# Keys' low half, LayerNorm statistics, four bias additions and unread products moved in the attention stage of a decoder layer

## What is computed

```python
# attention, on h = layernorm(x); 8 heads, 64 tokens to a sequence
c_q, c_kv = h @ W_DQ + b_DQ, h @ W_DKV + b_DKV          # 32 wide
q = concat(c_q @ W_UQ + b_UQ, c_q @ W_QR + b_QR)        # by head
k = concat(c_kv @ W_UK + b_UK, h @ W_KR + b_KR)
attn = softmax(einsum('bhsd,bhtd->bhst', q, k) * scale)
o = einsum('bhst,bhtd->bhsd', attn, c_kv @ W_UV + b_UV)
x = x + o.reshape(b, s, -1) @ W_O + b_O
# experts 1: router on the context, inputs layernorm(x)
logits = einsum('bsd,de->bse', context, Wg) + bg        # top 2 of 8, softmax
...
x = x + out
# experts 2: 8 of 32 from 4 of 8 groups, and shared ones
...
x = x + routed + shared
```

## Time and profile before

| what | value |
|---|---|
| median of three runs | 731.56 us (730.13 to 733.31) |
| profiled execution | 733.41 us, its span 731.6 us |
| PE busy | 651.0 us (89% of the span) |
| DVE busy | 548.4 us (75%) |
| ACT busy | 347.3 us (47%) |
| POOL busy | 345.7 us (47%) |
| mean granted clock of PE | 0.958 |

### The profile page before, as it was taken

One profiled execution on the slowest core, in us unless ns is written; L12 is line 12 of the kernel. 1 busy time (PEld: TensorE's weight loads), 2 busy tenths in 40 slices (PEclk: granted clock), 3 DMA queues, 4 the chain that ended last, 5 costly groups with the idle time before them and its releaser, 6 DMA issues. The chain is left out here.

```text
span 731.6 us, 10978 instructions
## 1 busy us (share of the span) xinstructions
PE 651.0 (89%) x3408; PEld 457.8 (63%) x3408; DVE 548.4 (75%) x1321; ACT 347.3 (47%) x633; POOL 345.7 (47%) x400
## 2 busy tenths in 40 slices
PE   8967888786669999999982998999999999999997
PEld 8635555554657777777761755666666666666664
DVE  4777888889248999999964786877868695958564
ACT  3845577653025666666663434344343435253221
POOL 5223787777758999999956423050403122000000
PEclk9978999999889999999995999999999999999999
DMA  8900130000133566676211474454544545353442
GB/s 215 381 27 1 46 93 30 33 30 38 44 101 112 168 178 204 179 196 178 79 58 44 99 164 118 111 138 115 135 114 123 142 122 138 90 141 110 128 115 58
DMA packets 74871, 84.13 MB, mean 115 GB/s; under 512 B 15345, under 2 KB 43995, under 8 KB 74814
## 3 DMA queue, kind: packets, MB, share of 16 engines
q1 hardware_dynamic: 69688, 74.93, 37.1%
q0 software_dynamic: 4288, 8.40, 3.9%
q10 hardware_dynamic: 838, 0.11, 0.1%
HBM read 64.48 MB, written 18.87 MB: 114 GB/s over the span
## 5 line engine op out<-in xcount | busy, mean ns | idle before, releaser
L883 ACT ACTIVATE r_s<-bank 128x512 f32<-128x512 f32 x136 | 81.0, 597 | 149.6 <-PE bank L1457 136.9
L1677 PE MATMUL pair_banks<-t_s,Dn 128*128 128x512 f32 x272 | 137.9, 592 | 0.7 <-issue 0.7
L1192 DVE TENSOR_TENSOR h1l<-r,h1h 128x512 fp32r<-128x512 f32 x92 | 113.0, 1246 | 18.1 <-POOL h1h L610 18.1
L1307 DVE TENSOR_TENSOR rc_s<-r_s,score_banks 128x512 f32<-128x512 f32 x90 | 61.5, 683 | 47.9 <-ACT r_s L883 29.5
L1455 PE MATMUL bank<-fxh,Gh 128*128 128x512 f32 x136 | 95.1, 699 | 0.0
L1320 DVE TENSOR_TENSOR t_s<-rc_s,bcb 128x512 f32<-128x512 f32 x128 | 87.4, 685 | 3.7 <-DMA bcb<-c_rows 3.0
L610 POOL TENSOR_SCALAR h1h<-r 128x512 fp32r<-128x512 f32 x92 | 73.5, 803 | 21.7 <-ACT r L829 19.7
L629 POOL TENSOR_TENSOR mvp<-mvp,meps 128x4 f32<-128x4 f32 x8 | 1.6, 197 | 170.0 <-DVE mvp L1230 170.0
L549 POOL DMA_INDIRECT x_sorted<-xsb,posi x64 | 63.6, 994 | 28.3 <-DVE xsb L1106 15.3
L621 POOL DMA_INDIRECT yg<-y_sorted,posi x64 | 62.9, 983 | 24.9 <-issue 18.4
L1677 PEld LDWEIGHTS pair_banks<-t_s,Dn 128*128 128x128 f32 x272 | 51.4, 190 | 16.0 <-issue 5.0
(11 more groups left out here) (295 smaller groups left out, 1575.2 us busy)
## 6 DMA issues: line engine op xcount, KB each, us to landing
bcb<-c_rows SPq DMA_DIRECT2D x128, 256.0 KB
wraw<-in_L_xattn_W SPq DMA_DIRECT2D x46, 256.0 KB
x_sorted<-wraw SPq DMA_DIRECT2D x1, 5888.0 KB, 19.1
xg<-x_sorted SPq DMA_DIRECT2D x23, 256.0 KB, 3.5
y_sorted<-ysb SPq DMA_DIRECT2D x23, 256.0 KB, 3.0
ctxb<-in_ctx SPq DMA_DIRECT2D x8, 256.0 KB, 4.6
out<-x_all SPq DMA_DIRECT2D x8, 256.0 KB
x_all<-in_x SPq DMA_DIRECT2D x2, 512.0 KB, 6.1
```

Of the source, the lines that this page charges most:

```text
L883: act.activation(r_s[:, n % RB2, :], bank[n % 3][:, :], ACT.Silu).then_inc(F["act"], 1)
L1192: tt(h1l[:, n % NB1, :], r1[:, n % RB1, :], h1h[:, n % NB1, :].bitcast(F32), ALU.subtract)\
L1307: tt(rc_s[:, n % CB2, :], r_s[:, n % RB2, :], bank[3 + n % 3][:, :], ALU.mult).then_inc(F["rc"], 1)
L1677: mm(bank[6][:, :], Dn[:, weights_of(p), :], t_s[:, n % TB2, :], start=(p == 0), stop=(p == NC2 - 1))\
```

## The change

- `kvlo` has offset -4 instead of -3 and stands behind `maximum` in the step, ahead of the context copy, the statistics, the router's piece and the bias. For group 1 it stood ahead of the maximum of n = 0 and now stands behind it. It waits for `kvS` alone (a new semaphore `kvs`), and PE's keys wait for the second copy as well.
- The statistics of tiles 16 to 31, which stood at n = -1, 0, 5 and 6, stand at n = -4, -3, -2 and -1. There is one part for them instead of two, so one power on POOL less. It stands ahead of the loop.
- `load_x(2)` goes ahead of the output weights, and both behind the small loads; the second half of the context comes after them.
- The bias addition of groups 0 to 3 goes from DVE (n = 4, 8, 12, 16) to POOL (n = 4 to 7).
- The unread products at the start are 5, 2 and 3 instead of 14, 4 and 8. Four new ones stand at n = 2.
- The lags stay as they are.

```diff
@@ -54,16 +54,17 @@
 HEAD = dict(xn=((-12, 0), (-11, 1), (-9, 2), (-9, 3)), xT=((-7, 0),), xh=((-6, 0),), xl=((-6, 0),), kv=((-5, 0),),
-            cq=((-5, 0),), kvS=((-4, 0),), cqS=((-3, 0),), kvlo=((-3, 0),),
+            cq=((-5, 0),), kvS=((-4, 0),), cqS=((-3, 0),), kvlo=((-4, 0),),
             keys=((-3, 0), (-3, 1), (-2, 2), (-2, 3)), kst=((-2, 0), (-2, 1), (-1, 2), (-1, 3)), v=((0, 0),), vh=((1, 0),))
...
 TAIL = 10
+PB = 4
 NV = NT - 3
...
 CTX = dict(turn=(-6, -4, -3, -2), copy=(-4, -3, -2, -1), product=(-3, -2, -1, 0), read=(-2, -1, 0, 1), back=(1, 2))
-PARTS = ((0, 4), (4, 8), (8, 16), (16, 24), (24, 32))
+PARTS = ((0, 4), (4, 8), (8, 16), (16, 32))
@@ -317,7 +318,7 @@
         A = {n: sem("at_" + n) for n in (
-            "xn xo xT xh xl kv_ps kvh kv cq_ps cq k_ps kst v_ps vh s_ps max sm exp sum rden p pv pT_ps ph "
+            "xn xo xT xh xl kv_ps kvs kvh kv cq_ps cq k_ps kst v_ps vh s_ps max sm exp sum rden p pv pT_ps ph "
             "u_ps uh o_ps x1 bst mva eps rstd xs").split()}
@@ -370,14 +371,14 @@
                 load_ctx(i)
-            sp.dma_start(wo_a[:, :, :], W_O.rearrange("(h k) d -> k h d", h=H)).then_inc(s_wo, 16)
             for dst, src in ((wg_a[:, 0:E1], Wg), (brow[:, :], row(bg)), (gbrow[:, :], row(gate_bias)),
...
                 sp.dma_start(dst, src).then_inc(s_small, 16)
+            load_x(2)
+            sp.dma_start(wo_a[:, :, :], W_O.rearrange("(h k) d -> k h d", h=H)).then_inc(s_wo, 16)
             for i in range(4, NS):
                 load_ctx(i)
-            load_x(2)
             sp.wait_ge(s_ctx[NQ - 1], 32)
@@ -563,18 +564,26 @@
+            def add_out_bias(m):
+
+                pool.wait_ge(A["xn"], m + 1)
+                xr = x_all[:, m * TPS:(m + 1) * TPS, :]
+                pool.tensor_tensor(xr, xr, obb[:, :].unsqueeze(1).to_broadcast([P, TPS, D]), ALU.add).then_inc(A["xo"], 1)
+
+            rstd1(3)
             for n in range(NT + TAIL):
...
                     normalise_p(m)
-                if n == 1:
-                    rstd1(3)
-                if n == 7:
-                    rstd1(4)
-                    router1_positions()
+                if n == 4:
+                    pool.wait_ge(s_N, 2)
+                if 4 <= n < 4 + PB:
+                    add_out_bias(n - 4)
                 m = n - LAG["rstd"]
...
                     rstd_pair(m)
+                if n == 7:
+                    router1_positions()
                 m = n - LAG["scatter"]
@@ -723,7 +732,7 @@
                         act.wait_ge(s_bias, N_BIAS)
-                    act.activation(kvS[:, q, :], bank[2][:, :], ACT.Identity, bias=bkv[:, :])
+                    act.activation(kvS[:, q, :], bank[2][:, :], ACT.Identity, bias=bkv[:, :]).then_inc(A["kvs"], 1)
                     act.activation(ckvD[:, q, :, :, :], bank[2][0:DC, :].rearrange("p (b s) -> p b s", s=S).unsqueeze(2)
@@ -962,15 +971,14 @@
             def statistics_rest(n):
+                if n == -4:
+                    dve.wait_ge(s_xin[2], 16)
+                if -4 <= n <= -1:
+                    statistics(32 + 4 * n, 36 + 4 * n)
                 if n == -1:
-                    dve.wait_ge(s_xin[2], 16)
-                if n in (-1, 0, 5, 6):
-                    first = {-1: 16, 0: 20, 5: 24, 6: 28}[n]
-                    statistics(first, first + 4)
-                if n in (0, 6):
-                    variance_eps(3 if n == 0 else 4)
-                if n in (3, 8):
-                    negated_mean1(3 if n == 3 else 4)
+                    variance_eps(3)
+                if n == 2:
+                    negated_mean1(3)
@@ -1075,8 +1083,6 @@
-                if m == 0:
-                    dve.wait_ge(s_N, 2)
                 dve.wait_ge(A["xn"], m + 1)
@@ -1088,7 +1094,7 @@
                 if name == "kvlo":
-                    dve.wait_ge(A["kvh"], m + 1)
+                    dve.wait_ge(A["kvs"], m + 1)
                     at = kvS[KV:2 * KV, q, :]
@@ -1133,11 +1139,6 @@
                     residual1(o)
-                if n == 0:
-                    head("kvlo", 1, 0)
-                for name, j, part in head_steps(n, ("kvlo",)):
-                    if j != 1:
-                        head(name, j, part)
                 if 0 <= u < NT:
@@ -1161,13 +1162,13 @@
                     maximum(n)
-                for step in head_steps(n, ("xl",)):
+                for step in head_steps(n, ("xl", "kvlo")):
                     head(*step)
...
                 router1(n)
-                if n % TPS == 0 and 4 <= n < NT + 4:
+                if n % TPS == 0 and PB <= (n - 4) // TPS < NS:
                     add_out_bias((n - 4) // TPS)
@@ -1362,14 +1363,14 @@
             pe.wait_ge(s_ident, 1)
-            unread(bank[6], 14)
+            unread(bank[6], 5)
             pe.wait_ge(s_heads, 16 * 6)
-            unread(bank[6], 4)
+            unread(bank[6], 2)
             pe.wait_ge(s_hqk, 2)
@@ -1383,7 +1384,7 @@
             ins.then_inc(s_gps, 1)
-            unread(bank[6], 8)
+            unread(bank[6], 3)
@@ -1483,6 +1484,7 @@
                         pe.wait_ge(A["kv"], m + 1)
+                        pe.wait_ge(A["kvh"], m + 1)
                         if m == 0:
@@ -1582,6 +1584,8 @@
                     out_absorbed()
+                if n == 2:
+                    unread(bank[0], 4)
                 if n == 3:
...
                 if n == 5:
```

## The result

The changed kernel takes 728.7 us (median of 20 executions, 724.17 to 732.9) against 731.56 for the kernel before (20 executions, 730.13 to 735.15): a ratio of 0.9954 with a 95% interval of 0.9938 to 0.9970, so 3.4 us less (the two medians by themselves differ by 2.9). The forecast was 723.2, or 8.4 less. The direction and the range held; the likeliest case was more than twice too large. The profiled execution took 730.11 us (span 728.4); its counterpart took 733.41 (731.6). The ratios in this document leave out three executions in a slower state, one of 830 us (ten products, `fill_keys2`) and two of 739 (`fill_five`, the profiled one among them).

A forecast was written before the change was run, and what follows sets the result against it. PE was taken to set the pace from 20 to 38 us, DVE from 38 to 45 and 62 to 76, neither from 45 to 62. 5.6 us by n = 9 plus 2.8 steady made 8.4: 723.2 us, range 718.5 to 729.5.

The forecast's parts named there:

- Head: Start, up to the first key product: fewer unread products bring it 1.2 us earlier (bounds 0 and 2.5); first scores 0.2 late.
- first batch: Unread products at the very start, 14 cut to 5: at most 1.7 us gained, 0.5 net taken.
- Low half of group 1: n = 1 to 4: keys wait for the low half behind the maximum; 1.2 us later, with the head's 0.2 1.4 late.
- Low half of group 2: Ahead of the router's piece, near 50 us: low half 2.5 us earlier, less the 1.4, makes 1.1 early.
- The clock: PE from 45 to 62 us: full clock worth 3.5 us, no change 0; half taken, 1.8, so 2.9 early at n = 6.
- Statistics, positions: n = 5 to 9: statistics gone from DVE, one power off POOL, positions 1.8 earlier; together 2.0 to 3.5 us, 2.7 taken.
- Steady part: 80 to 176 us: PE's four waits for the keys' low half, 4.2 us in all, shrink; 2.8 us gained.
- The bias on POOL: n = 4 to 7, four additions of 1.04 us on POOL: zero effect, with 3.2 us for collisions with DVE in the range.
- (a): Rival: clock stays at half through the ranks and the stretch at 76, steady waits move elsewhere; 727.0 us, chance 0.17.
- (d): Rival: x load at n = -4 lands late and holds up copies, then PE; 727.0 us at landing 24.9, 736 at 34; chance 0.06.
- (b): Rival: POOL's scatter chain takes the pace from the first scatter on, nothing left of the steady 2.8; 726.0 us, chance 0.14.

The follow-up runs named there:

- fill_keys2: The changed kernel with ten more unread products on PE at n = 5, ahead of the keys of group 2: ratio 0.9880 to the kernel before.
- fill_five: The changed kernel with five unread products on PE at n = 5, ahead of the keys of group 2: ratio 0.9943 to the kernel before.
- three bias kernels: The changed kernel with all bias additions on DVE (0.9981), those of groups 4 to 7 left out (0.9917), or those one step later, ahead of the maximum (0.9910).
- low order alone: The kernel before with only the keys' low half of every group moved behind the maximum (offset -4): ratio 1.0054 to the kernel before.

## Why the prediction was right or wrong

**Head (1.2 earlier at the first key product): 0.7.** The landing was underrated (4.54, not 6), the slow clock was underrated more. No run shows the 0.5 that the sum takes for the first batch: PE started 3.1 us earlier and then needed 13.4 us to the first key product where it had needed 11.0, and in other traces of the same head this second number is 11.7 to 14.4. The copy of the context was foreseen behind the low half; I had its end at 21.1 and it came at 21.7. What that costs I had right: 1.4 us from the first key product to the first scores, measured 1.4 (14.80 us to the first maximum, before 13.37). So the first maximum came 0.7 late instead of 0.2 for the smaller gain ahead of it.

**Low half of group 1 (loop 1.4 late at n = 1 to 4): 2.1, then 3.1.** The first part by the mechanism told. The last 1.0 is the router's comparison beside POOL's bias. I had priced such meetings at zero with 3.2 in the range, on the ground that the steps next to it read PSUM. That one does not, and 1.0 was lost at once. Here the Trainium skill's rule (GPSIMD Engine Reference, Key points: GpSimd shares SBUF interfaces with VectorE and contends with instructions with two SBUF inputs) was the better guide; I had given it some 3 us and set it aside. The rows at 45.63 and 127.13 and those of the three bias kernels agree with it.

**Low half of group 2 (2.5 earlier).** Right as a term: from n = 4 to 5 the loop took 6.42 us where it took 8.82, 2.4 less.

**The clock (1.8): this step failed.** I took half of 3.5 for a partial cure and it was nothing: 9.14 us from n = 5 to 6, before 8.66. The reason given, that the gap shrinks from 3.56 to 2.9, fell with the late n = 4 (3.51 measured). It would not have been enough either: the gap is 1.61 us with the bias on DVE and 1.15 with the low order alone, and the key product behind it still takes 0.75 and 0.74, since the clock is down before the gap begins. The whole was mis-sized as well. With the fill, n = 0 to 6 takes 27.7 us instead of 32.1 (34.03 to 61.73, 32.76 to 64.87), 4.4 less where I had 3.5, and n = 6 to 9 takes 13.0 instead of 14.6, another 1.6. I had priced the keys, the ranks and the next round, not every pass up to n = 9.

**Statistics, positions (2.7): 1.9** from n = 6 to 9 (14.62 us, before 16.48). Right in kind. As one part alone it carries the whole result.

Together, n = 9: 0.7 + 1.3 + 1.0 - 2.4 + 0.5 - 1.9 = -0.8 (measured -0.7), where I had -5.6.

**Steady part (2.8): 0.6 by n = 31.** The waits did go: the steps 16 to 17 and 20 to 21 of PE's scores took 4.69 and 4.68 us, before 5.47, and 24 to 25 took 4.69, before 6.80. But steps 22 to 23 took 6.89 instead of 4.96 and 27 to 28 took 5.16 instead of 3.08. The step of the reasoning that failed was to count the waits of PE and not to ask where the instructions on DVE behind the moved one would land: the addition, 0.68 us alone, landed on POOL's normalisation and took 1.58, with POOL's scatter waiting for the scaling behind it. It is not all of the loss: 1.5 of the 1.9 us in step 22 to 23 is PE at its lower level, and so is much of step 27 to 28, where PE's rows are slow from 156.9 to 163. The prediction had no falls of the clock behind 80 us. With the additions ahead of the maximum the granted clock is 1.00 from 80 to 160 us.

**The bias on POOL (zero).** Zero alone (0.9994), but not in the new order: it costs 1.0 at n = 4 and spares collisions of DVE, for some 2 us net in its favour.

Of the rivals, (a) is what came about, by its two reasons at once: the clock stayed at half through the ranks, and the steady waits moved elsewhere. It gave 727.0; the collision at n = 4 (1.0) and the smaller gain at the head (0.5) make most of the rest. Rival (d), a late x load, didn't occur at all. (b), POOL's chain as pace setter, is not what the rows say: POOL still waited 12.4 us for DVE between 80 and 176:

```profile
POOL x_sorted L550 <- DVE xsb L1112: 12.4, 14, 2.5
```

**What stays open.** The changed kernel's executions spread over 8.7 us, those before over 5.0. The head's two courses can be a part of that: with the old numbers of unread products twelve executions spread over 5.1. Another cause can be read but was not tried by itself: in kernels that keep both of PE's new gaps (2.13 us at 21.75, 1.01 at 35.02), three of six traces have part of the half level between 33 and 42 us as well. The change and the kernel with the bias ahead of the maximum, in that stretch:

```profile
33.00:42.00 9.00, 7.20 (x62) 4.50 (x52) 6.91 (x15) 6.92 (x14) 3.29 (x2) 1.00 0.75 286
...
33.00:42.00 9.00, 7.98 (x49) 4.01 (x40) 4.28 (x8) 6.27 (x13) 3.30 (x2) 0.62 0.70 268
```

Up to step 20 the second is the same program, and its first maximum starts at the same time (32.77), but its third starts at 42.0, 2.8 us later. The Trainium skill (TensorE: Matmul & The Clock Gate, Part 1) says that the point at which the gate acts varies from run to run; these two rows agree. The six kernels made from the change with the low half of group 1 ahead show 1.00 there. But the two kernels with the statistics moved in the old order, which have neither gap, show it as well (0.86 and 0.84), so the gaps can't be the whole cause. How often the change meets it no run counted. Also open are where the clock falls in those executions of the low order alone that have no trace, and 1 us of the result that arises between n = 31 and the expert stage and 1 us behind it.

## What to carry to other kernels

A moved step must be priced by what lands where it was: write down which instruction will stand beside the other engine's SBUF work, not only which wait goes. Unread products in a gap of PE can give back more than they cost, but try more than one number of them (here ten gave 5.4 us and five nothing), and try them again after each other change: in the old order the same ten gave 1 us or less. Look for the clock's level at every step that got slower before blaming a wait. A bundle whose parts were never run alone can hide a part that costs as much as another gives: here 5.7 us of gain beside an order that alone costs 4. One trace isn't the kernel: look at the same stretch in all kernels that share its code.

## What the hardware showed

- DVE's 128x512 addition of two SBUF tensors takes 0.68 us alone and 1.58 (change) to 2.19 us (low order alone) beside POOL's tensor operation; a 128x128 scaling goes from 0.34 to 1.07 and 1.25, a 128x256 comparison from 0.42 to 1.44. POOL's own normalisation stays at 1.05. The slowed instruction ends 0.1 to 0.6 us after POOL's.
- POOL's bias addition takes 1.27 us, the normalisation of the same shape 1.04.
- Ten unread 128x128 products in a PE gap of 3.5 us hold the full clock for the first keys behind it, or bring it back (their twenty passes took 2.40 to 3.82 us), and give 5.4 us in the changed kernel; five give nothing that can be measured. In four of the seven kernels with the ten, the clock fell once more within 10 us. Where the gap was 1.15 or 1.61 us by itself, the clock was down before it and stayed down behind it.
- Starting PE's work on the head weights at 4.54 instead of 7.68 us brought the first key product forward by 0.7, since its products took 1.92 us a set instead of 1.09. With 14, 4 and 8 unread products the way from one to the other took 10.97 to 10.99 us in nine traces, with 5, 2 and 3 it took 11.7 to 14.4 in ten.
- A slowed step of the loop (22 to 23) took 5.4 us in three traces and 6.9 in three others with the same instructions there, the difference being PE's clock.
